# Moving the delta chain of the next chunk two half steps earlier in a fused Mamba and MLP kernel

## What is computed

```
h = rmsnorm(layernorm(x)) * norm_w
u, z = split(h @ in_proj.T)                       # 512 channels each
uc = silu(conv_b + sum_k up[:, k:k+L] * conv_w[:, k])   # 4 taps
dt, B, C = split(uc @ x_proj.T)                   # 16, 16, 16
delta = softplus(dt @ dt_proj.T + dt_b)
h_t[d,n] = exp(delta*A[d,n]) * h_(t-1)[d,n] + delta*B[n]*uc[d];  y_t[d] = sum_n C[n]*h_t[d,n]
out = ((y + uc*D) * silu(z)) @ out_proj.T         # then residual, layernorm, residual
h = silu(x@w1 * s1) * (x@w2 * s2); h = gelu(h@h1 * ..); h = gelu(h@h2 * ..); out = h@w3 * ..
```

## Time and profile before

| | us |
|---|---|
| Median of three runs | 2046.79 |
| The profiled execution's own time | 2048.19 |
| Its span, first to last instruction | 2046.4 |
| PE busy with matmuls | 1482.2 (72%) |
| DVE busy | 1412.6 (69%) |
| ACT busy | 1272.0 (62%) |
| POOL busy | 1056.4 (52%) |
| Mean granted TensorE clock | 0.843 of full speed |

### The profile page before, as it was taken

One profiled execution on the slowest core, in us unless ns is written; L12 is line 12 of the kernel. 1 busy time (PEld: TensorE's weight loads), 2 busy tenths in 40 slices (PEclk: granted clock), 3 DMA queues, 4 the chain that ended last, 5 costly groups with the idle time before them and its releaser, 6 DMA issues.

```text
span 2046.4 us, 29755 instructions
## 1 busy us (share of the span) xinstructions
PE 1482.2 (72%) x9080; PEld 1295.6 (63%) x9080; DVE 1412.6 (69%) x2378; ACT 1272.0 (62%) x2766; POOL 1056.4 (52%) x746
## 2 busy tenths in 40 slices
PE   4666677777768777776777777686787777686865
PEld 2122566666757666675766776685676667576765
DVE  3678876777677767776777677676767776677510
ACT  4354665766566676767567675766657665766444
POOL 0435474645547465564647455464746556475322
PEclk8787878888888887898888988798788888878877
DMA  3222100101010010101001010110001010000000
GB/s 109 88 88 62 32 17 20 35 23 33 24 32 23 17 34 22 36 19 33 24 17 38 17 39 18 33 28 30 21 17 38 22 33 22 27 22 21 14 7 6
DMA packets 38919, 63.64 MB, mean 31 GB/s; under 512 B 5216, under 2 KB 19424, under 8 KB 38640
## 3 DMA queue, kind: packets, MB, share of 16 engines
q10 hardware_dynamic: 18944, 33.83, 5.4%
q1 hardware_dynamic: 19696, 26.02, 3.9%
HBM read 55.38 MB, written 4.46 MB: 29 GB/s over the span
## 4 chain that ended last, share of the span: by engine, by line
PE 28%; DVE 21%; ACT 19%; issue 18%; POOL 12%; ACTq 1%; DVEq 1%; POOLq 0%; DMA 0%; SPq 0%
DVE S L1095 7%; PE fP L561 7%; PE fP L562 6%; POOL S L439 6%; PE sT L585 4%; DVE hP L1155 3%; ACT dA L815 3%; PE fP L549 3%; PE hP L549 3%; POOL Glo L500 3%; DVE acc L1109 3%; ACT o L847 1%; ACT L999 1%; PE hP L626 1%; ACT Rw L993 1%
## 5 line engine op out<-in xcount | busy, mean ns | idle before, releaser
L439 POOL TENSOR_TENSOR S<-X,Bs 128x1024 f32<-128x1024 f32 x256 | 606.9, 2371 | 639.3 <-PE sT L585 440.2
L1095 DVE TENSOR_TENSOR_SCAN S<-dA,S 128x512 f32<-128x512 f32 x512 | 622.4, 1216 | 214.3 <-ACT dA L815 111.6
L815 ACT ACTIVATE dA<-delta,A 128x255 f32<-128x255 f32 x1024 | 445.3, 469 | 510.5 <-DVE S L1095 458.1
L561 PE MATMUL fP<-Ghi,w_h 128*128 128x256 f32 x2048 | 564.2, 310 | 80.6 <-DVE z L1186 52.1
L562 PE MATMUL fP<-Glo,w_h 128*128 128x256 f32 x2048 | 538.1, 297 | 0.0
L561 PEld LDWEIGHTS fP<-Ghi,w_h 128*128 128x128 f32 x2048 | 421.8, 206 | 94.6 <-DVE z L1186 47.7
L585 PE MATMUL sT<-ident,S 128*128 128x128 f32 x2048 | 358.3, 309 | 141.3 <-DVE acc L1109 121.8
L562 PEld LDWEIGHTS fP<-Glo,w_h 128*128 128x128 f32 x2048 | 421.8, 206 | 0.0
L1109 DVE SCALAR_TENSOR_TENSOR acc<-sT,CT,acc 128x512 f32<-128x512 f32 x480 | 349.6, 731 | 104.2 <-PE sT L585 104.0
L585 PEld LDWEIGHTS sT<-ident,S 128*128 128x128 f32 x2048 | 273.5, 159 | 215.7 <-DVE acc L1109 131.9
L500 POOL TENSOR_TENSOR Glo<-Rw,Ghi 128x1024 fp32r<-128x1024 f32 x96 | 226.1, 2357 | 178.1 <-ACT Ghi L995 96.7
(11 more groups left out here) (132 smaller groups left out, 2023.4 us busy)
## 6 DMA issues: line engine op xcount, KB each, us to landing
Bs<-b_rows ACTq DMA_DIRECT2D x128, 256.0 KB, 3.1
Rw<-in_h SPq DMA_DIRECT2D x11, 512.0 KB, 3.2
xh<-in_x SPq DMA_DIRECT2D x16, 256.0 KB, 4.0
xt<-in_x SPq DMA_DIRECT2D x16, 256.0 KB, 4.0
out<-x SPq DMA_DIRECT2D x16, 256.0 KB, 2.7
x<-in_h SPq DMA_DIRECT2D x5, 512.0 KB, 3.2
Rw<-in_w SPq DMA_DIRECT2D x4, 512.0 KB, 4.5
w_in<-in_in_proj SPq DMA_DIRECT2D x1, 1024.0 KB, 5.6
```

The source lines that it names most:

```text
L439: pool.tensor_tensor(s[:, :, :], X[par][:, :, :], row[:, None, :].broadcast_to([P, DT, T]), ALU.mult).then_inc(scan_pool.sem, 1)
L561: pe.matmul(dst, w[:, i, cols_], hi[:, i, :], start=(j == 0), stop=False)
L815: a = act.activation(dA[half][:, i, 1:], delta[par][:, d, 1:], ACT.Exp, scale=A[:, d * N + n:d * N + n + 1])
L1095: a = dve.tensor_tensor_scan(pair, dA[half][:, :, :].rearrange("p d t -> p (d t)"), pair, 0.0, ALU.mult, ALU.add)
```

## The change

The chain of the head is moved to earlier half steps on every engine. x_proj on PE goes from 20 to 19, the transposes and dt_proj from 22 to 21; ACT's `xdbl` copy from 21 to 20, `store_B` and the copy of C from 22 to 21, relu and abs from 23 and 24 to 22 and 23, exp from 24 to 23, Ln from 26 to 24; DVE's rest from 25 to 24; POOL's two sums from 27 to 25, `first_decay` and `X` from 29 to 26, and `carried` from 30 to 29. In the SiLU stretch `uc` comes first. The exponential of `first_decay` leaves `front` and goes to ACT's hs 28. The loads of B stay at 24 and 28.

```diff
@@ pool head_step @@
-                if hs == 27:
+                if hs == 25:
                     pool.wait_ge(head_vec.sem, head_vec.at(h, "res"))
...
-                if hs == 29:
+                if hs == 26:
                     pool.wait_ge(head_pool.sem, head_pool.at(h, "delta"))
...
-                if hs == 30:
+                if hs == 29:
                     carry_in(h, 0, first)
@@ pe head_step @@
-                if hs == 20:
+                if hs == 19:
                     pe.wait_ge(head_act.sem, head_act.at(h, "silu1"))
...
-                if hs == 22:
+                if hs == 21:
                     pe.wait_ge(head_act.sem, head_act.at(h, "dtx"))
@@ act front @@
                 if half == 0 and n == 0:
-                    act.wait_ge(head_pool.sem, head_pool.at(c, "first_rate"))
-                    act.activation(first_decay[:, :, :], first_decay[:, :, :], ACT.Exp).then_inc(head_act.sem, 1)
                     act.wait_ge(gaps_zero, 2)
@@ act head_step @@
-                if hs == 21:
+                if hs == 20:
                     act.wait_ge(head_pe.sem, head_pe.at(h, "xp"))
...
-                if hs == 22:
+                if hs == 21:
                     store_B(h, hp)
-                if hs == 22:
+                if hs == 21:
                     act.wait_ge(head_pe.sem, head_pe.at(h, "cT"))
...
-                if hs in (23, 24):
+                if hs in (22, 23):
-                    q = hs - 23
+                    q = hs - 22
...
-                if hs == 24:
+                if hs == 23:
                     act.wait_ge(head_act.sem, head_act.at(h, "v1"))
...
                 if hs in (24, 28):
                     load_B(h, hp, (hs - 24) // 4)
-                if hs == 26:
+                if hs == 24:
                     act.wait_ge(head_vec.sem, head_vec.at(h, "res"))
...
+                if hs == 28:
+                    act.wait_ge(head_pool.sem, head_pool.at(h, "first_rate"))
+                    act.activation(first_decay[:, :, :], first_decay[:, :, :], ACT.Exp).then_inc(head_act.sem, 1)
@@ act silus @@
+                if head:
+                    act.wait_ge(head_vec.sem, head_vec.at(h, "tap2"))
+                    for q in range(2):
+                        act.activation(uc[hp][:, 2 * q:2 * q + 2, :], hP[(q + 1) % 2][:, :, :],
+                                       ACT.Silu).then_inc(head_act.sem, 1)
                 if tail:
...
                 if head:
-                    act.wait_ge(head_vec.sem, head_vec.at(h, "tap2"))
-                    for q in range(2):
-                        act.activation(uc[hp][:, 2 * q:2 * q + 2, :], hP[(q + 1) % 2][:, :, :],
-                                       ACT.Silu).then_inc(head_act.sem, 1)
                     act.wait_ge(head_act.sem, head_act.at(h, "z1"))
@@ dve head_step @@
-                if hs == 25:
+                if hs == 24:
                     dve.wait_ge(head_act.sem, head_act.at(h, "e"))
```

## The result

The changed kernel takes 2074.09 us (median of 4 runs, 2072.93 to 2074.98), the kernel before 2047.44 beside it (4 runs). The ratio is 1.013, with a 95% interval of 1.0112 to 1.0147. The forecast of 2048.0 was too low by 26 us, and the time lies outside the range of 2037 to 2060. Busy times hardly moved (PE 1488.0 us, DVE 1420.6, ACT 1275.7, POOL 1058.9), and the granted clock is 0.837, where it was 0.843. The profiled execution's span grew from 2046.4 to 2073.2, by 26.8.

What follows compares the result with a forecast made beforehand. The prediction took the order of work as the bound, with ACT's wait for `first_decay` on a path through POOL's product 15. First passes -3.0, boundaries 0 and clock +4.2 gave +1.2, so a median of 2048.0, range 2037 to 2060.

Steps and rivals of the forecast that it cites:

- POOL: POOL's step at a chunk boundary: its chain ends 5.1 us earlier, but product 15 behind it ends at 1108.1 instead of 1102.85.
- Then follows h1_5's copy: End of the POOL step: after ACT's dA at 1110.2 come h1_5's copy and 3.21 us to the GELU, at 1113.45.
- that sum: Sum of one boundary, SiLU to GELU: 38.2 us against a mean of 38.20 before, so 0 in the mean.
- Two half steps on paper are one microsecond: ACT's way to exp: its queue is full, so exp begins just 0.97 us before its old time.
- Clock term: PE's lower clock after new idle time: 0 to 1.0 us per boundary, taken as 0.3, so 14 x 0.3 = +4.2.
- the sign for it: Sign of a wrong forecast: granted clock clearly below 0.84, with stretches of matmuls 0.21 apart from h1_2 on.
- PE loses its clock in the new pause: Slower rival at h1_2 to h1_4: 1.0 us at each of 14 boundaries, 2058; with two blocks 2077. Chance 0.25.
- The third rival: Slower: product 15 still later, as POOL waits for Ln behind a late rest; each 0.5 us is 7, 2054. Chance 0.10.
- the faster rival: The chain is shorter than added: 0.4 to 1.0 us gained at each of 14 boundaries, 2030 to 2038. Chance 0.28.
- First passes: Gains before the steady boundaries: -1.5 from PE's counting matmuls in the first pass, -1.5 at chunk 0's boundary; -3.0 together.
- The other -1.5: At the boundary of chunk 0, DVE's 1.88 us wait for product 0 shrinks: 0 to -1.9, taken as -1.5.
- ACT waits some 1.5 us for the rest here, while nobody needs it: ACT's Ln at a boundary waits for DVE's rest; the prediction gave this wait no cost.

## Why the prediction was wrong

- **The failed step is in "POOL"**, in the words "Then follows h1_5's copy": I let ACT wait for product 15 at half step 30 only, through dA and DVE's scan. ACT has an earlier wait for the same product at 28, ahead of `load_B`, that I had not in the sum, though the text of the change says that the loads stay. Where I forecast 38.2 it made 39.4: +1.2 in each of 14 passes. With the load at 30 the interval is 38.2 to 38.5 wherever the clock stays up, so the rest of that sum held.
- Right, at the same boundary: exp at 17.6 behind the SiLU load (1109.19 - 1091.60), L478 at 22.5, product 15 done 1108.1 - 1075.26 = 32.8 behind it (1124.42 - 1091.60), the pause of PE ahead of h1_2 (1.87). "Two half steps on paper are one microsecond" was borne out on ACT.
- **Clock term**: 4.2 was forecast at h1_2 to h1_4, as a clock that is seldom lost ("I take 0.3"). It was lost in eight of 14 passes, and the sign for it (matmuls 0.21 apart from h1_2 on) is there. Its price of 1.0 was right: with the load at 30 the two passes that lose it are 0.9 to 1.1 longer. In the changed kernel it added nothing, because the wait for the load covers it, but without that wait eight such passes would cost some 9 us (my estimate, 8 x 1.1). So the rival "PE loses its clock in the new pause" was right about the event in more than half of the passes and had its cost hidden. A further 4.4 came behind the GELU, a place I had not looked at. The third rival (product 15 later) was wrong: product 15 came at its forecast time. Nothing of the faster rival came.
- **First passes**: of the -3.0, the part of the first pass is there in about its size (the first product of chunk 0 at 55.71 after 57.05, -1.3 for -1.5). The other -1.5 is not. Against it stand 7.6 us in the pass for chunk 0, of which 6.0 are DVE's stretched comparisons, which the sum had not.
- Two readings of the prediction are off without touching the sum. `first_decay` begins 7.6 us after product 15 and is finished after 8.0 (1107.79 + 0.43 - 1100.20). And the slots are given as the reason why the intervals of before alternate; three slots under 16 states would repeat after three chunks and not after two, so the reason is not shown.
- I had priced "ACT waits some 1.5 us for the rest here, while nobody needs it" at nothing. That holds only where product 15 is last and sets the interval anyway. With product 15 ahead of the chain, rest and Ln at 24 instead of 25 cost 3.6 a pass (39.99 against 36.37).

What stays open: the clock's choice, for which I have no rule (next but one section), and with it why moving the load left two passes with a lost clock instead of eight.

## What to carry to other kernels

When an instruction that others wait for is moved back, list every wait on its semaphore in every queue, DMA issues of compute engines included: a load that reuses a buffer waits for the last reader and holds all that is queued behind it. A wait moved ahead of work that somebody needs is not free even where its result is early: place it directly behind that work, as Ln behind h1_0's copy. If undoing one part brings nothing back, try it together with the other parts. POOL's order undone brought nothing with Ln at 24, but with rest and Ln moved to 25 as well the time fell by 49 us (2074.2 to 2025.1). And look at every pass: a cost that stands under a longer wait does not show in the time, and comes out when the wait is taken away.

## What was unexpected of the hardware

- A wait of a DMA issue on ACT stands in the profile's waits with the next computing instruction, here 49.1 us at the exponential, with POOL's L442 as what ended it.
- What a pause of PE does to its clock. Ahead of h1_2, the seven kernels that have the pause there (98 passes) show pauses of 1.05 to 2.02 with the granted clock at 1.00 behind them (46), and pauses of 2.07 to 2.56 with 0.57 to 0.71 over the next 4 us (52), with no exception. Ahead of h1_7, in the kernel with the load at 30 and Ln at 25, the length does not decide: four pauses of 2.56 to 2.59 kept the clock, as did two of 1.88 and 1.92; six of 2.54 to 2.66 and two of 2.39 lost it. Both came in one kernel, pass by pass, so a single pass says little.
- A DVE `tensor_tensor` on SBUF tiles was held until POOL's running instruction had ended, 1.8 to 2.1 us for one of 1.23. Where it had started first, POOL's instruction was held, 3.31 for 2.40.
